# An adaLN layer with gated linear attention and eight experts on one core: expert rows scattered home, tiles in pairs, packed projections

## The chip, the cores and the metric

One of the eight cores of a Trainium2 chip runs the whole program. The metric is the time of one execution in microseconds of the device (us), shorter being better. Engines are called as the profile calls them: PE (matrix products), PEld (its weight loads), DVE, ACT and POOL (elementwise work), SP (issues transfers). All data are 32-bit floats, and each matrix product appears as two records in the trace.

## The reference

Input `x` is (2, 1024, 256). With a modulation `mod` of a small vector `c`:

```python
mod = (_silu(L0_c) @ L0_wmod).reshape(L0_c.shape[0], 6, 1, -1)
ga = (2 * (ga >= 0) - 1) * jnp.maximum(jnp.abs(ga), 0.25)   # gb likewise
x = x + ga * attn(_layernorm(x) * (1 + ca) + sa)
x = x + gb * ffn(_layernorm(x) * (1 + cb) + sb)
```

`attn` is gated linear attention: 16 heads of 16, chunks of 64 tokens, projections q, k, v, an output gate, and decay gates `log_sigmoid(x @ Wg1 @ Wg2 + bg2) / 16` of low rank 16. `ffn` routes each token to the best two of 8 experts (width 176, `silu(h1) * h2` between `up` and `proj`), weighs their results by softmax probabilities, and adds a shared expert of width 704 times a sigmoid gate.

## The kernel before, in words

Tokens stand in 16 tiles of 128, four tiles to a block of 512. The text calls the pass `s` of the main loop a slot. Five stages follow each other.

1. **Attention (slots 0 to 4).** Slot `s` projects block `s` (G the output gate, V, K, Q) and makes block `s-1`'s scores, masks, outputs and output projection (WO), block `s-2`'s layer norm, transposes (HT) and router. Near its end a slot transposes the next block, makes its low-rank product (LR, lines 1222 and 1352) and its gate logits (Z, line 1357), then the key-value sums (KV, line 1395). The products of a slot go through two PSUM banks, `work0` and `work1`, in turn: `unit_order` lists the units, and `begin` makes PE wait until the unit two before has been read. Scores go to four banks `at_ps`, outputs to `o_even` and `o_odd`. DVE masks the scores (line 978) and ACT evacuates and makes the exponentials.
2. **Shared expert.** For a block the parts are six "up" parts (line 1192: units SA and SB, two products of 512 columns each; the sixth has only 64 hidden features) and two "down" parts (line 1202). `FILL_PLACES` puts the parts of blocks 0 to 2 into gaps of slot 4 and of the routing.
3. **Routing and scatter.** DVE computes for each token and choice a row in a table sorted by expert (`pos_u`, line 822), each expert's rows filled up to whole tiles of 128. POOL writes `h2tok` rows to those places in DRAM with 32 indirect transfers (line 523). Meanwhile PE works off the remaining shared parts (the place "scatter").
4. **Experts.** 40 tiles of 128 sorted rows are loaded back in pairs (SP, line 400). For each tile PE transposes the rows (line 1494), makes both up products with the weights of the tile's expert, which it reads by a register (line 1510, 352 columns), transposes the hidden values (line 1518, two halves of 88) and multiplies down (line 1525, 256 columns, 88 rows of the array). DVE copies the result (line 1121) and SP stores it, still sorted, to `ys_sorted` (line 406).
5. **Tail.** POOL gathers two rows for each token (line 532, 32 indirect transfers), DVE weighs and adds them (lines 1159 to 1168), and SP stores the tile (line 421). PE makes block 3's whole shared part beside it.

```python
            pe.wait_ge(y_out, ETILES)
            for f in range(FTS):
                shared_up(pe, t_, begin, NBLK - 1, f)
```

At the start POOL clears `vpad` and `atm` (lines 437 and 438), then makes the masks, and signals `const_pool` behind the last (line 471). PE waits for it ahead of its first transposes (line 1346).

## Time and profile before

| | |
|---|---|
| median of three runs | 502.7 us (502.02 to 503.12) |
| the profiled execution's own time | 501.09 us |
| its span, first to last instruction | 499.1 us |
| PE busy | 433.5 us, 87% of the span |
| DVE, ACT, POOL busy | 238.8, 137.4, 110.1 us |
| mean granted clock of PE | 0.921 of full |

The engines run side by side and wait for each other by semaphores, so a busy share does not tell what ends last. A stage is read by its windows, its waits and the chain of waits that ended last. The span is 2.0 us shorter than the execution's time, for what lies around it.

### The profile page before, as it was taken

The page shows a single profiled execution, that of the slowest core. Times are in us where ns is not written, and L with a number is a line of the kernel's source. Part 1 is how long each engine was busy: PE and PEld are TensorE (multiplying, and loading weights), DVE is VectorE, ACT ScalarE, POOL GpSimd, SP SyncE. Part 2 cuts the span into 40 slices and gives each one's busy share as a digit, 9 for nine tenths or more (in the row PEclk, how much of TensorE's full clock was granted, in tenths as well). Part 3 has the DMA queues.
Part 4 walks back from the last instruction along what each step waited for, and adds up shares of the span by engine and source line. Part 5 has one row for each costly group of instructions (what it writes and reads, how often), then busy time and mean ns, then how long its engine had stood idle before and what let it go on. Part 6 is the DMA issues. An engine that isn't in the chain of part 4 may idle for free.

```text
span 499.1 us, 9641 instructions
## 1 busy us (share of the span) xinstructions
PE 433.5 (87%) x3860; PEld 269.4 (54%) x3861; DVE 238.8 (48%) x573; ACT 137.4 (28%) x277; POOL 110.1 (22%) x134
## 2 busy tenths in 40 slices
PE   2798799999999998997999896758999999997466
PEld 2344465558456666634645642525777777752134
DVE  4054395487749569112543621021444444437467
ACT  2285413643743521161113110002222222210000
POOL 9203000510321051010000177700000000027742
PEclk9989878979988998799999999956999999998869
DMA  8990000000000000092000022330242434225533
GB/s 281 319 385 11 3 3 3 0 3 4 3 1 4 3 1 3 3 255 94 0 0 1 11 95 105 106 105 0 87 125 89 123 90 120 75 73 147 148 95 95
DMA packets 31248, 38.29 MB, mean 77 GB/s; under 512 B 3481, under 2 KB 28394, under 8 KB 31210
## 3 DMA queue, kind: packets, MB, share of 16 engines
q1 hardware_dynamic: 28138, 29.35, 18.7%
q0 software_dynamic: 3072, 8.39, 5.4%
q8 instruction: 29, 0.48, 0.4%
q14 instruction: 9, 0.07, 0.1%
HBM read 20.95 MB, written 16.78 MB: 76 GB/s over the span
## 4 chain that ended last, share of the span: by engine, by line
PE 68%; DVE 11%; issue 6%; ACT 5%; POOL 5%; another core or an unknown queue 3%; DMA 1%; DVEq 0%; POOLq 0%
PE work L1192 11%; PE at_ps L1510 10%; PE work L1222 8%; PE work L1525 7%; PE work L1202 7%; PE at_ps L1255 4%; PE work L1380 3%; PE work L1337 3%; PE at_ps L1494 2%; PE at_ps L1243 2%; PE work L1357 2%; PE o_even L1305 1%; PE work L1328 1%; PE work L1395 1%
## 5 line engine op out<-in xcount | busy, mean ns | idle before, releaser
L1202 PE MATMUL work<-sdn_sb,hs 128*128 128x256 f32 x192 | 52.8, 420 | 12.5 <-issue 6.7
L1510 PE MATMUL at_ps<-arena 128*128 x160 | 56.8, 478 | 1.3 <-ACT arena L748 1.1
L1202 PEld LDWEIGHTS work<-sdn_sb,hs 128*128 128x128 f32 x192 | 36.2, 202 | 30.2 <-issue 16.9
L523 POOL DMA_INDIRECT xs_sorted<-h2tok,pos_u x32 | 31.3, 979 | 73.5 <-DVE pos_u L822 64.1
L900 DVE TENSOR_TENSOR hs<-work,hs 128x512 f32<-128x512 f32 (+1 forms) x24 | 16.5, 689 | 64.0 <-PE work L1192 39.8
L1192 PE MATMUL work<-h2T,sup_sb 128*128 128x512 f32 (+1 forms) x96 | 45.1, 619 | 0.6 <-DVE hs L900 0.3
L532 POOL DMA_INDIRECT er_neg<-ys_sorted,pos_u x16 | 15.5, 969 | 128.5 <-DMA ys_sorted<-er_pos 119.7
L1525 PE MATMUL work<-arena 88*128 x160 | 41.1, 380 | 0.0
L545 ACT ACTIVATE hs<-work 128x512 f32<-128x512 f32 (+1 forms) x24 | 14.3, 596 | 90.4 <-PE work L1192 61.3
L1510 PEld LDWEIGHTS at_ps<-arena 128*128 128x128 f32 x160 | 31.1, 196 | 13.6 <-issue 3.5
L1192 PE MATMUL work<-hT,sup_sb 128*128 128x512 f32 (+1 forms) x48 | 25.5, 680 | 14.3 <-DVE hs L900 11.8
L752 ACT ACTIVATE arena<-at_ps 128x176 f32<-128x176 f32 x40 | 12.7, 318 | 77.2 <-PE at_ps L1510 77.2
L486 POOL TENSOR_TENSOR sq<-sq,sg 128x512 f32<-128x512 f32 x8 | 10.0, 1274 | 101.2 <-issue 101.2
L1192 PEld LDWEIGHTS work<-h2T,sup_sb 128*128 128x128 f32 (+1 forms) x96 | 17.2, 187 | 24.8 <-issue 22.4
L1525 PEld LDWEIGHTS work<-arena 88*128 88x128 f32 x160 | 27.2, 190 | 2.4 <-issue 0.2
L1192 PEld LDWEIGHTS work<-hT,sup_sb 128*128 128x128 f32 (+1 forms) x48 | 9.1, 201 | 29.4 <-issue 15.0
L1255 PE MATMUL at_ps<-arena 32*64 32x128 f32 x512 | 22.1, 349 | 2.8 <-issue 1.6
L748 ACT ACTIVATE arena<-at_ps 128x256 f32<-128x256 f32 x40 | 15.4, 384 | 30.3 <-PE at_ps L1494 30.1
L1192 PE MATMUL work<-za,sup_sb 128*128 128x512 f32 (+1 forms) x48 | 21.0, 596 | 1.3 <-DVE tmp L908 1.3
L908 DVE SCALAR_TENSOR_TENSOR tmp<-work,sgate,rows 128x256 f32<-128x256 f32 x16 | 7.0, 479 | 31.1 <-remote 19.8
L1121 DVE COPY er_pos<-work 128x256 f32<-128x256 f32 x40 | 17.0, 425 | 9.4 <-PE work L1525 9.4
L1222 PE MATMUL work<-hT,wgate_sb 128*128 128x512 f32 x32 | 20.8, 808 | 0.7 <-ACT za L622 0.7
(196 smaller groups left out, 730.8 us busy)
## 6 DMA issues: line engine op xcount, KB each, us to landing
xs_sorted<-arena SPq DMA_DIRECT2D x10, 512.0 KB, 7.8
h2tok<-xs_sorted SPq DMA_DIRECT2D x20, 256.0 KB, 2.8
ys_sorted<-er_pos SPq DMA_DIRECT2D x20, 256.0 KB, 2.2
arena<-in_e_up SPq DMA_DIRECT2D x8, 352.0 KB
x_sb<-in_x SPq DMA_DIRECT2D x4, 512.0 KB, 8.5
out_rows<-xn SPq DMA_DIRECT2D x16, 128.0 KB
sup_sb<-in_s_up SPq DMA_DIRECT2D x1, 1408.0 KB, 6.4
arena<-in_e_down SPq DMA_DIRECT2D x8, 176.0 KB
```

What stands on the lines that cost most here:

```text
L523: g.indirect_dma_start(out=xs_dram, out_offset=bass.IndirectOffsetOnAxis(ap=pos_u[:, k, t:t + 1], axis=0), in_=h2tok[:, t, :], in_offset=N ...
L532: g.indirect_dma_start(out=gath_sb[k][:, t % 4, :], out_offset=None, in_=ys_dram, in_offset=bass.IndirectOffsetOnAxis(ap=pos_u[:, k, t:t + ...
L748: a.activation(xT[:, u % 2, :], at_ps[u % 2][:, 0:KC * P], ACT.Copy).then_inc(xT_ready, 1)
L900: v.tensor_tensor(hs[0:m, f, :], bank(("SB", blk, f))[0:m, :], hs[0:m, f, :], ALU.mult).then_inc(hs_ready, 1)
L1121: v.tensor_copy(yout[:, (u // 2) % 2, u % 2, :], work[u % 2][:, 0:HID]).then_inc(y_out, 1)
L1192: ins = t_.matmul(o[0:m, :], sup_sb[:, k, w, f0:f0 + m], h2T_of[blk][:, k, :], start=(k == 0), stop=(k == KC - 1))
L1202: ins = t_.matmul(o[:, t * HID:(t + 1) * HID], hs[0:m, f, tk], sdn_sb[0:m, f, :], start=(f == 0), stop=(f == FTS - 1))
L1222: ins = t_.matmul(o[0:rows_, :], w[:, k, gr * P:gr * P + rows_], rhs[:, k, :], start=(k == 0), stop=(k == KC - 1))
L1255: ins = t_.matmul(at_ps[j][CHUNK * e:CHUNK * (e + 1), q * P:(q + 1) * P], kh[r, gr, c * CHUNK:(c + 1) * CHUNK], qeo[r, gr, c, :, :].rearra ...
L1337: ins = t_.matmul(o[:, t * HID:(t + 1) * HID], hT[:, k, tk], wv_sb[:, k, :], start=(k == 0), stop=(k == KC - 1))
L1510: ins = t_.matmul(at_ps[2 + u % 2][:, 0:2 * FE], xT[:, u % 2, k * P:(k + 1) * P], eup[:, bass.ds(e, 1), k, :].rearrange("p a n -> p (a n)" ...
L1525: ins = t_.matmul(work[u % 2][:, 0:HID], hTe[0:FEH, u % 2, k * P:(k + 1) * P], edn[0:FEH, bass.ds(e, 1), k, :].rearrange("p a n -> p (a n) ...
```

## The change

It has nine parts. Line numbers of code after it are those of the changed file.

1. **Start.** POOL makes the identity first and signals it by itself (`ident_ready`). PE's first transposes wait for that alone. `vpad` and `atm` are cleared behind `const_pool`. SP issues more small loads (four copies of `wg2`, two of `bg2`) and the shared up weights in four transfers.
2. **Packed LR and Z.** LR is four products of 32 weight columns, each in its own quarter of the output rows. Z is two products of 64 array rows each, one per half of the array. Z goes to `at_ps[2]` and `at_ps[3]` and is no longer a unit of `work`.
3. **Block order.** Half of G now stands ahead of the first scores, and V ahead of HT. The modulation rows of batch 0 are finished in slot 0 and those of batch 1 in slot 2.
4. **Packed sixth up part.** SA and SB of the last 64 features are one product of 128 columns.
5. **Four early up parts.** Four of block 3's six up parts move from the tail to the place "scatter".
6. **Wider rows.** A sorted row has 263 numbers in place of 256. Among the seven more are its token, its weights and its batch. The probabilities are made ahead of the positions.
7. **Pairs of expert tiles, 39 of 40.** Hidden transposes of two tiles fill one bank and are copied at once. The down product is split into 128 and 48 rows of the array in place of twice 88. For the second tile of a pair the 48 rows stand at 64 to 111, with weights that ACT copies there.
8. **Scatter home.** POOL computes each sorted row's place from its extra columns (five small operations per pair), DVE multiplies the expert's result by the token's weight and the `gb` row while it copies it out of PSUM, and POOL writes it to its token's row with one indirect transfer per tile.
9. **Tail.** SP loads both tables of rows back, eight transfers of 512 KB. DVE adds two times per pair of token tiles and SP stores.

```diff
-    both("Z", 0)
@@ main loop, PE
             for s in range(NBLK + 1):
+                if s < NBLK:
+                    project(("G", s, 0), wgate_sb, 0, hT)
                 if b >= 0:
                     scores_first(b)
                 if s < NBLK:
-                    for gr in range(KC):
-                        project(("G", s, gr), wgate_sb, gr, hT)
+                    project(("G", s, 1), wgate_sb, 1, hT)
@@ low_rank, gate_logits
-                project(("LR", s, 0), wg1_sb, 0, hT, LOWR)
+                for gr in range(KC):
+                    for k in range(KC):
+                        r = slice(32 * (2 * gr + k), 32 * (2 * gr + k) + 32)
+                        ins = t_.matmul(o[r, :], wg1_sb[:, k, :], hT[:, k, :], start=True, stop=True)
-                    o = begin(("Z", s, gr))
-                    t_.matmul(o[:, :], wg2_sb[:, gr * P:(gr + 1) * P], tT[:, :], start=True, stop=True).then_inc(unit_full, 1)
+                    r = slice(64 * gr, 64 * gr + 64)
+                    t_.matmul(at_ps[2 + gr][:, :], wg2_sb[r, gr * P:(gr + 1) * P], tT[r, :], start=True, stop=True
+                              ).then_inc(z_full, 1)
@@ shared_up
+            if f == FTS - 1:
+                o = begin(("SA", blk, f))
+                for k in range(KC):
+                    ins = t_.matmul(o[:, :], sup_tail[:, k, :], h2T_of[blk][:, k, :],
+                                    start=(k == 0), stop=(k == KC - 1))
+                return
@@ fill and tail
+EARLY_UP = 4
+SHARED_PARTS += [("U", NBLK - 1, f) for f in range(EARLY_UP)]
-            for f in range(FTS):
+            for f in range(EARLY_UP, FTS):
                 shared_up(pe, t_, begin, NBLK - 1, f)
@@ experts, PE
+            def down(i, q, w, e, tiles=2):
+                pe.wait_ge(hTe_ready, q + 1)
+                at_least(pe, y_out, i, 0)
+                for t in range(tiles):
+                    t_.matmul(work[t][:, 0:HID], hTe[:, w % 2, t * P:(t + 1) * P],
+                              edn[:, 0, bass.ds(e[t], 1), :].rearrange("p a n -> p (a n)"), start=True, stop=False)
+                ins = t_.matmul(work[0][:, 0:HID], hTe[0:FE1, w % 2, 2 * P:3 * P],
+                                edn[0:FE1, 1, bass.ds(e[0], 1), :].rearrange("p a n -> p (a n)"), start=False, stop=True)
+                if tiles == 2:
+                    pe.wait_ge(odd_ready, q + 1)
+                    r = slice(CHUNK, CHUNK + FE1)
+                    ins = t_.matmul(work[1][:, 0:HID], hTe[r, w % 2, 3 * P:4 * P], edn_odd[r, w % 2, :],
+                                    start=False, stop=True)
@@ experts, POOL
+            def put_rows(q):
+                for u in range(min(2, ETILES - 2 * q)):
+                    i = 2 * q + u
+                    pool.wait_ge(y_out, i + 1)
+                    g.indirect_dma_start(out=ys_dram, out_offset=bass.IndirectOffsetOnAxis(ap=goal_u[:, i:i + 1], axis=0),
+                                         in_=yout[:, q % 2, u, :], in_offset=None, bounds_check=TOPK * TOK - 1,
+                                         oob_is_err=False).then_inc(ys_stored[i % 4], 16)
+            for q in range(EPAIRS):
+                if q + 2 < EPAIRS:
+                    goals(q + 2)
+                put_rows(q)
@@ experts, DVE
+            def row_gains(i, u):
+                    v.scalar_tensor_tensor(out=row_gain[:, t, :], in0=row_step, scalar=goal[:, (u // 2) % XPAIRS, t, 2:3],
+                                           in1=rows[:, 0, GB, :], op0=ALU.mult, op1=ALU.add).then_inc(gain_ready, 1)
+            def evac_y(i0, q0, u):
+                dve.wait_ge(down_full, q0 + u // 2 + 1)
+                dve.wait_ge(gain_ready, i0 + u + 2 - u % 2)
+                v.scalar_tensor_tensor(out=yout[:, (u // 2) % 2, u % 2, :], in0=work[u % 2][:, 0:HID],
+                                       scalar=goal[:, (u // 2) % XPAIRS, u % 2, 1:2], in1=row_gain[:, u % 2, :],
+                                       op0=ALU.mult, op1=ALU.mult).then_inc(y_out, 1)
@@ tail, SP and DVE
+            for q in range(NBLK):
+                for k in range(TOPK):
+                    r0 = k * TOK + q * BLK
+                    sp.dma_start(yin[:, q, k, :, :], ys_dram[r0:r0 + BLK, :].rearrange("(t p) c -> p t c", p=P)
+                                 ).then_inc(ld_y[q], 16)
+            def combine(n):
+                t = 2 * n
+                steps.did(v.tensor_tensor(y0, y0, y1, ALU.add))
+                xv = x_sb[:, t:t + 2, :]
+                v.tensor_tensor(xv, y0, xv, ALU.add).then_inc(comb_done, 2)
```

**Where a slot turns over, PE.** Before, from LR's neighbour to the outputs from the state (`hT,wg_sb` is LR, `tT,wg_sb` is Z, `arena,xn` is KV, `at_ps<-arena` the scores, `wgate_sb` G):

```order
L1222 MATMUL work<-hT,wg_sb 16x512 x2
L1380 MATMUL work<-wo_sb,yT 128x256 x4
L1357 MATMUL work<-tT,wg_sb 128x512 x2
L1395 MATMUL work<-arena,xn 32x32 x64
L1255 MATMUL at_ps<-arena 64x128 x32
L1222 MATMUL work<-hT,wgate_sb 128x512 x4
```

After:

```order
L1463 MATMUL work<-hT,wg_sb 32x512 x4
L1499 MATMUL work<-wo_sb,yT 128x256 x4
L1475 MATMUL at_ps<-tT,wg_sb 128x512 x2
L1514 MATMUL work<-arena,xn 32x32 x64
L1325 MATMUL work<-hT,wgate_sb 128x512 x2
L1360 MATMUL at_ps<-arena 64x128 x32
L1325 MATMUL work<-hT,wgate_sb 128x512 x2
```

LR has four products in place of two, Z leaves `work`, and half of G has come between KV and the scores.

**One expert tile, PE, before** (`ISA` reads a register; `arena` holds weights and hidden values):

```order
L1510 ISA
L1510 MATMUL at_ps<-arena 128x352
L1510 ISA
L1510 MATMUL at_ps<-arena 128x352
L1494 MATMUL at_ps<-ident,h2tok 128x128 x2
L1518 MATMUL o_even<-ident,arena 88x128 x2
L1525 ISA
L1525 MATMUL work<-arena 128x256
L1525 ISA
L1525 MATMUL work<-arena 128x256
```

After, half of a pair's turn (up of the second tile, its successor's transposes, the down products of the pair in front):

```order
L1630 MATMUL at_ps<-arena 128x352
L1630 ISA
L1630 MATMUL at_ps<-arena 128x352
L1614 MATMUL at_ps<-ident,h2tok 128x128 x2
L1648 REGISTER_ALU
L1651 ISA
L1651 MATMUL work<-arena 128x256
L1651 ISA
L1651 MATMUL work<-arena 128x256
L1653 ISA
L1653 MATMUL work<-arena 128x256
L1658 MATMUL work<-xn,arena 128x256
```

Four down products serve two tiles as before, but the last two stand on different halves of the array. The hidden transposes of both tiles (lines 1640 and 1643) stand once per pair, ahead of this piece.

**The same stage, POOL, after** (before, POOL has nothing there); one pair's goals, then two scatters of the pair two before:

```order
L565 TENSOR_SCALAR second<-h2tok,texp 128x1 [waits ld_xt3]
L565 TENSOR_SCALAR second<-h2tok,texp 128x1
L568 TENSOR_TENSOR turned<-h2tok,second 128x6 [waits pool_step]
L571 TENSOR_TENSOR goal<-turned,h2tok 128x6 [waits pool_step]
L574 TENSOR_SCALAR goal_u<-goal 128x2 [waits goal_ready]
L582 DMA ys_tokens<-er_pos,goal_u 4096x256 [waits y_out,pool_step]
L582 DMA ys_tokens<-er_pos,goal_u 4096x256 [waits y_out]
```

Five small operations and two indirect transfers per pair have moved into a stage in which POOL was idle.

**The tail, DVE.** Before, one token tile behind one of block 3's up parts:

```order
L900 TENSOR_TENSOR hs<-work,hs 128x512 [waits unit_full,silu_done]
L1159 TENSOR_SCALAR er_neg<-er_neg,pw 128x256 [waits out_stored0,gath0]
L1161 SCALAR_TENSOR_TENSOR er_neg<-gk,pw,er_neg 128x256 [waits dve_step]
L1163 TENSOR_TENSOR er_neg<-er_neg,rows 128x256 [waits dve_step]
L1168 TENSOR_TENSOR xn<-er_neg,x_sb 128x256 [waits dve_step]
```

After, the last two up parts and the first four token tiles:

```order
L984 TENSOR_TENSOR hs<-work,hs 128x512 [waits unit_full,silu_done]
L984 TENSOR_TENSOR hs<-work,hs 64x512 [waits silu_done]
L1263 TENSOR_TENSOR arena<-arena 128x512 [waits ld_y0]
L1269 TENSOR_TENSOR x_sb<-arena,x_sb 128x512 [waits dve_step]
L1263 TENSOR_TENSOR arena<-arena 128x512
L1269 TENSOR_TENSOR x_sb<-arena,x_sb 128x512 [waits dve_step]
```

Four operations per token tile have become two per pair of tiles, and they wait for loads instead of gathers.

## Rows read from the trace of the kernel before

**Rows 1.** The page: the span, and GB/s moved in its 40 equal slices.

```profile
span 499.1 us, 9641 instructions
...
GB/s 281 319 385 11 3 3 3 0 3 4 3 1 4 3 1 3 3 255 94 0 0 1 11 95 105 106 105 0 87 125 89 123 90 120 75 73 147 148 95 95
```

**Rows 2.** Windows of six stages: length, then busy us (instructions) of PE, PEld, DVE, ACT, POOL, clock, DMA.

```profile
0.00:61.40 61.40, 43.84 (x305) 23.19 (x306) 21.38 (x47) 28.84 (x46) 18.37 (x38) 0.95 0.61 203
61.40:107.30 45.90, 42.76 (x717) 26.82 (x709) 31.35 (x60) 18.19 (x34) 8.54 (x10) 0.83 0.01 2
...
211.60:284.80 73.20, 67.98 (x224) 37.47 (x224) 28.59 (x89) 19.90 (x31) 2.49 (x2) 1.00 0.21 60
284.80:336.40 51.60, 37.93 (x97) 19.30 (x97) 10.36 (x18) 3.58 (x6) 31.33 (x32) 0.85 0.30 102
336.40:442.30 105.90, 104.16 (x480) 77.57 (x480) 43.72 (x120) 24.39 (x80) 0.00 (x0) 0.96 0.29 87
442.30:499.10 56.80, 37.48 (x96) 17.52 (x96) 33.57 (x76) 3.58 (x6) 31.23 (x32) 0.88 0.40 116
```

**Rows 3.** Waits of PE over the span: waiter <- releaser: total us, times, longest.

```profile
PE work L1346 <- POOL qsel L471: 5.3, 1, 5.3
...
PE work L1395 <- ACT za L622: 2.2, 3, 0.7
PE work L1395 <- issue: 2.0, 1, 2.0
...
PE at_ps L1255 <- DVE arena L978: 1.1, 1, 1.1
```

**Rows 4.** Timeline of PE in slots 2 and 3: start, us, engine, line, x records.

```profile
99.66 1.98 PE L1357 MATMUL work<-tT,wg_sb 33*128 33x512 f32 x4
...
107.27 4.84 PE L1222 MATMUL work<-hT,wgate_sb 128*128 128x512 f32 x8
...
113.95 2.59 PE L1255 MATMUL at_ps<-arena 32*64 32x128 f32 x64
...
140.35 1.89 PE L1222 MATMUL work<-hT,wg_sb 128*16 128x512 f32 x4
```

**Rows 5.** Timeline of PE, shared parts of 64 and of 128 weight columns.

```profile
224.72 3.17 PE L1192 MATMUL work<-h2T,sup_sb 128*64 128x512 f32 x7
...
247.08 8.85 PE L1192 MATMUL work<-h2T,sup_sb 128*128 128x512 f32 x20
```

**Rows 6.** Timeline of the fill stage: POOL's first and last scatter, SP's loads, PE.

```profile
284.85 1.21 POOL L523 DMA_INDIRECT xs_sorted<-h2tok,pos_u  x1 [64.09 <-DVE pos_u L822]
...
324.66 0.96 POOL L523 DMA_INDIRECT xs_sorted<-h2tok,pos_u  x1 [0.30 <-issue]
...
327.09 1.91 SPq L400 DMA_DIRECT2D h2tok<-xs_sorted  x4
...
328.93 0.58 PE L1202 MATMUL work<-sdn_sb,hs 128*128 128x256 f32 x1 [0.82 <-issue]
...
330.33 4.08 PE L1202 MATMUL work<-sdn_sb,hs 128*128 128x256 f32 x8 [0.82 <-issue]
```

**Rows 7.** Chain that ended last, in order of time, one expert tile.

```profile
436.48 0.86 PE work L1525 x4
437.35 1.19 PE at_ps L1510 x4
```

**Rows 8.** Lines with their shapes, 347.8 to 437.3 us: 36 tiles.

```profile
L1121 DVE COPY er_pos<-work 128x256 f32<-128x256 f32 x36 | 15.3, 425 | 7.9 <-PE work L1525 7.9
```

**Rows 9.** Lines of POOL over the span: a small operation.

```profile
L495 POOL TENSOR_TENSOR f_all<-f_base,f_last 128x16 f32<-128x16 f32 x4 | 0.9, 220 | 0.0
```

**Rows 10.** Timeline of the tail: DVE behind its longest wait, POOL beside DVE, DVE's last.

```profile
477.16 0.69 DVE L900 TENSOR_TENSOR hs<-work,hs 128x512 f32<-128x512 f32 x1 [8.20 <-remote]
...
486.45 1.15 POOL L532 DMA_INDIRECT gk<-ys_sorted,pos_u  x1 [0.30 <-issue]
```

**Rows 11.** Timeline of DVE: the last instruction before the last store.

```profile
495.69 0.69 DVE L921 TENSOR_TENSOR xn<-x_sb,tmp 128x512 f32<-128x512 f32 x1
```

More of the change, by code:

```diff
@@ L387, in _ @@
             sp.wait_ge(zero_ready, 5)
-            for i in range(ETILES // 4):
+            for i in range(ESLOTS // 4):
                 sp.dma_start(xs_dram[i * BLK:(i + 1) * BLK, :].rearrange("(t p) c -> p t c", p=P),
@@ L461, in _ @@
                                           base=0, pattern=[[0, 2 * NPAIR], [1, CHUNK]], channel_multiplier=-1))
+            for j in range(0, NPAIR, 2):
+                steps.sync()
+                steps.did(g.affine_select(out=lr_bias[:, :], in_=lr_bias[:, :], compare_op=ALU.not_equal, fill=1.0,
+                                          base=-(32 * j + LOWR), pattern=[[0, 1]], channel_multiplier=1))
             steps.sync()
@@ new lines, in _ @@
+            dve.wait_ge(y_ready, 2 * NBLK)
+            steps.did(v.tensor_tensor(row_step, rows[:, 1, GB, :], rows[:, 0, GB, :], ALU.subtract))
+            steps.sync()
+            group(0, 0, first=True)
+            with dve.Fori(1, ESLOTS // EGRP - 1) as grp:
+                group(grp * EGRP, grp * XPAIRS)
+            group(ESLOTS - EGRP, ESLOTS // 2 - XPAIRS, tiles=ETILES - ESLOTS + EGRP)
+            evac_hT(EPAIRS - 1, XPAIRS - 1)
+            row_gains(ETILES - 1, EGRP - 2)
+            y_slot_free(ESLOTS - EGRP, EGRP - 2)
```

489 lines of the change are left out of this document (273 added, 216 removed).

## Prediction

> **What bounds the kernel now.** I read the page for the span, then the windows by stage, then in each stage the waits, the timeline and the chain. The span is 499.1 us [rows 1]. The windows say where it goes [rows 2]: slots 0 and 1 (61.4 and 45.9 us), the routing after slot 4 (73.2), the fill (51.6), the experts (105.9) and the tail (56.8). PE is busy 104.16 of 105.9 us in the experts, 67.98 of 73.2 in the routing and 42.76 of 45.9 in slot 1, so there PE's own work sets the time. It is busy only 37.93 of 51.6 in the fill and 37.48 of 56.8 in the tail, at clocks of 0.85 and 0.88: these two stages wait. In the fill POOL issues scatters from 284.85 to 325.6 and SP loads the sorted rows from 327.09 [rows 6]. But PE is late too: at 328.93 it still makes the last down part, with 0.58 us per product record and idle time put down to "issue". In the tail POOL is busy 31.23 of 56.8 us with gathers, and DVE once waits 8.20 us for something that the profile cannot name [rows 10]. So four stages are to be judged by themselves, and the gains of stages in series add up.
>
> **The attention slots.** Part 1 takes away PE's wait for POOL's masks, 5.3 us [rows 3]. Nothing is queued there that could take its place: the small loads that SP now issues ahead are needed only after the first transposes. Bound from 3 to 5.3, I take 5.3.
>
> Part 2: LR and Z are four records each, 1.89 and 1.98 us [rows 4], though LR has 16 weight columns and Z 33 array rows, so narrowness alone saves nothing. Packed, LR is eight records in four quarters and Z four in two halves; side by side each lasts as long as two records, 0.95 us. Are they side by side? The scores say so: 64 records of 128 columns in 2.59 us are 0.040 us each [rows 4], while four records of 352 columns take 1.19 us [rows 7], which for 128 columns is 0.108 us each. That is 2.7 at a time. So I take 0.95 us off each of the eight (four blocks, two each), 7.6 in all. The bounds are 0 and 7.6.
>
> The Trainium skill, TensorEngine Tiling, section Key Properties, says the opposite can happen: changing the tiling mode drains TensorE. By that rule, with one drain per change, the packing could give back what it wins, and this is a rival below; the trace, with its dense scores, speaks for the gain.
>
> Part 3: KV no longer follows Z in the same banks, so its waits go: 2.2 us for ACT and 2.0 put down to issue [rows 3]. The modulation rows leave slot 1, where scores waited 1.1 us for DVE [rows 3]. Against this, half of G (four records, the eight of rows 4 took 4.84 us at a falling clock) now stands ahead of the scores, and DVE's masks start later by that. DVE is busy 31.35 of 45.9 us there [rows 2], much of it behind the scores. I give back 1 us in each of three slots. Sum: 5.3 + 7.6 + 2.2 + 2.0 + 1.1 - 3 = 15.2 us. The bounds are 6 (no packing gain, more given back) and 20.
>
> **Routing.** Part 4 drops four records for each block. Seven records of 64 weight columns take 3.17 us, 0.45 each, and twenty of 128 columns 8.85, 0.44 each [rows 5]; so width is free and 1.8 us goes per block. Blocks 0 and 1 stand ahead of the positions: 3.6 us. The probabilities now come ahead of the positions, but DVE waits there for PE's counts, so I cost them at nothing; uncovered, six operations of about 0.2 us are 1.2. The first scatter then starts at 284.85 - 15.2 - 3.6 = 266.0.
>
> **The fill.** Two floors. The scatters: 42.2 us from the first to the loads [rows 6], plus 1 MB of loads at 281 GB/s [rows 1], 3.7; together 46. A row of 1,052 bytes in place of 1,024 changes nothing here, since DMA engines are busy 0.30 of the stage [rows 2] and POOL's issue, 0.96 us and 0.30 before it, sets the pace. PE: an up part is eight records of 0.44, 3.5 us; a down part is 24, at 4.08/8 us each for half clock [rows 6], so 0.25 at full, 6.0. The place held three down and six up parts, 39 us, of which the first down part, 6.0, is done when the scatter starts; now it holds three down and 9.5 up, 51.3. Before, 51.6 us passed over 33 us of work: 19 us were lost, 2 of them the turn to the experts. With none lost the stage lasts 51.3 - 6.0 = 45, with all of it 64. Part of the loss was at the end, while the scatters and the loads ran, and would now lie elsewhere in PE's work. I take the middle, 55: the experts start at 321. The early parts are thus nearly free here, and what they cost if the scatters were no cover is 4 x 3.5 = 14 us, which the tail gives back.
>
> **The experts.** 36 tiles take 347.8 to 437.3 us [rows 8], 2.49 each, 4.97 a pair. Of it down is 0.86 per tile [rows 7]. The pair's two 48-row products stand on different halves and banks: four records in the time of two, 0.43 less, 4.54. The first two stay full. The transposes and ACT's copy of the odd weights change nothing: the copy's target is read a pair later. Nineteen pairs and one tile: 88.8. The stage before had 105.9 - 99.6 = 6.3 us for a cold start and its end; PE now comes to it warm, so 3.5. Stage 92.3, ending at 413.3.
>
> Whether others keep up: DVE has per pair two copies of 0.43 [rows 8] in their new form, two row gains alike, one copy of 512 columns (0.69 by [rows 11]) and two products of at most 0.43, 3.3 us of 4.54. POOL has two transfers of 1.26 and five operations of 0.22 [rows 9], 3.6 us with no gaps, 5.1 with 0.3 before each. It is the nearest to the bound. Who waits: DVE's copy for the slot that POOL empties, PE's next down product for that copy. Beside a busy DVE a transfer took 1.15 us in place of 0.96 [rows 10, 6]: 0.4 more for a pair, 4.0, still under 4.54.
>
> The Trainium skill, DMA: Bandwidth & Descriptors, section SWDGE vs HWDGE vs iDMA, has DVE lock GpSimd out of the memory that holds the descriptor rings during two-port operations. That is in line with the 1.15, and by it POOL's part would grow further than by the row.
>
> **The tail.** After the last copy: one scatter 0.96 and its landing 1.5 (325.62 to 327.09) [rows 6], 2.5; issue and first landing, 2 as an estimate from the same landing; 4.2 MB of loads, with 1.6 MB of stores among them, at 350 GB/s (between the 281 and 385 of [rows 1]) 16.6; the last block's two pairs of DVE operations, 4 x 0.69 [rows 11], 2.8; two last additions of the shared part, 2 x (0.43 + 0.43 + 0.69), 3.1; the last store, 499.1 less 496.4 [rows 1, 11], 2.7. Sum 29.8 in place of 56.8. PE's own work beside it, 1.5 up parts and two down parts, is 17 us and hidden. Bounds: 26 (loads at 385, stores free) and 36 (all at 250).
>
> **Sum.** 413.3 + 29.8 = 443.1 for the span. The profiled execution took 2.0 us more than its span, and the median of the runs stands 1.6 us above it (502.7 against 501.1). Forecast 447 us.
>
> **Rivals.** (A) Packing does not overlap, since each change between whole and divided array empties PE. Then eight times 0.95 and twenty times 0.43 are not saved, 16 us: 463. The scores speak against it; that they hardly ever leave the divided form speaks for it. Chance 0.12. (B) PE's losses in the fill vanish, since the rest of its work lies behind the last scatter. The experts then start at 312 to 314: 439. For it: the slow records stand at the end of the scatters. Chance 0.20. (C) POOL paces the experts at 5.1 to 5.9 us per pair, 12 to 27 us more: about 466. For it, the rows just named; against, small operations at 0.22 with nothing before them [rows 9]. Chance 0.10. (D) Slower than before: the landing of the scatters holds the two result slots. A slot is free when copy 0.9, two issues 2.5 and the landing L are over, and that has two pairs' time, 9.1 us; so it is hidden up to L = 5.7, and each microsecond more costs 0.5 per pair, 10 in all. With 55 us to lose it decides from L = 11. The landing seen is 1.5 [rows 6]. Price at L = 12: 510. Chance 0.04. (E) The new block order costs DVE's chain some 5 us in each slot: 462. Chance 0.04. Mine has 0.50, and 436 to 458 as its own range.
>
> **How the numbers follow.** Two runs of this kernel differ by some 0.2%, about 1 us, and I call that "same". All cases but (D) end far below 502.7. The range from 431 to 470 takes in A, B, C and E; it leaves out D and the far ends. Faster 0.94, same 0.01, slower 0.05.
>
> **What would show it.** Right: first transposes 5 us earlier; LR and Z of 1 us; first scatter near 266; experts from about 321 with 4.5 us per pair and no idle PE; last up part to last store 30 us. Wrong: a pair of 4.97 (A); DVE's copies released by POOL or by transfers (C, D); PE waiting for DVE's masks (E); or loads of 512 KB landing one after the other far below 300 GB/s in the tail.

## The result, and the profile after

Beside each other the changed kernel took 457.0 us (median of 6 runs, 452.9 to 459.1) and the kernel before 502.9 (501.5 to 508.6). The ratio is 0.907, with an interval of 0.901 to 0.913: 46 us less, where the forecast had 447 us and 56 less. Ratios, here and below, leave out a few executions with a lower granted clock that are over 1.5% longer than the fastest of their kernel, so they need not be the quotient of the medians. The profiled execution took 459.1 us over a span of 457.3; the forecast's span was 443.1. So 14.2 us are to be explained on the span, and, as the experiments show, some of it depends on the chip that the program runs on.

The page of the changed kernel, to be read against [rows 1]:

```profile
span 457.3 us, 9813 instructions
...
GB/s 262 296 309 240 3 5 1 3 3 4 0 3 4 1 1 4 2 268 114 0 0 0 2 47 106 107 106 106 0 83 105 89 122 97 84 92 47 32 313 238
```

The last two slices of GB/s are the loads and stores of the tail. Its windows, columns as in [rows 2], cut at the same points of the program as the later ones of [rows 2]: the fill in three pieces, and the tail.

```profile
266.00:286.00 20.00, 19.43 (x46) 8.27 (x45) 6.69 (x12) 2.98 (x5) 14.59 (x15) 1.00 0.25 88
286.00:313.00 27.00, 12.76 (x49) 8.61 (x48) 0.98 (x2) 0.59 (x1) 17.25 (x19) 0.80 0.35 117
313.00:331.00 18.00, 17.16 (x36) 7.56 (x36) 5.45 (x10) 2.69 (x6) 4.18 (x15) 0.83 0.08 27
...
430.00:457.30 27.30, 19.55 (x62) 11.28 (x61) 15.63 (x25) 1.19 (x2) 1.94 (x2) 0.91 0.72 234
```

The second piece of the fill is the one to look at: PE is busy 12.76 of 27 us, DVE 0.98, ACT 0.59, while POOL and the transfers go on as before. The timeline of that stretch, against [rows 6] (the stop of DVE first, then PE's slow records, then the loads; in brackets the idle time ahead and what ended it, "remote" being what the profile can't name):

```profile
286.84 0.69 DVE L984 TENSOR_TENSOR hs<-work,hs 64x512 f32<-64x512 f32 x1 [1.57 <-issue]
...
287.59 11.15 PE L1305 MATMUL work<-sdn_sb,hs 128*128 128x256 f32 x45 [1.41 <-DVE hs L984]
...
304.25 0.58 PE L1305 MATMUL work<-sdn_sb,hs 64*128 64x256 f32 x1 [2.32 <-issue]
...
309.83 21.57 SPq L421 DMA_DIRECT2D h2tok<-xs_sorted  x5
312.71 0.88 DVE L992 SCALAR_TENSOR_TENSOR tmp<-work,sgate,rows 128x256 f32<-128x256 f32 x2 [25.18 <-remote]
...
313.64 16.73 PE L1295 MATMUL work<-hT,sup_sb 128*128 128x512 f32 x32 [8.81 <-DVE tmp L992]
...
331.23 1.15 PE L1630 MATMUL at_ps<-arena 128*128 x3 [0.43 <-ACT arena L802]
```

PE has the first down part's 24 records done by 293.6, so DVE could copy then. It does so at 312.71, 2.9 us after SP's first load of sorted rows is issued. PE's last three records of the second part end 0.8 to 2.9 us apart in place of 0.25 (each lasts 0.4 to 0.6, the rest is idle time ahead of it), and then its next bank waits for DVE. All 32 records of the early up parts stand behind that, 313.64 to 330.2. The experts start at 330.2, not at 321.

What did DVE wait for in those 19 us? The chain of waits over the same stretch (start, us, what) says that it was a signal, and when the signal came:

```profile
286.88 25.81 another core or an unknown queue
312.69 0.03 issue
312.71 0.89 DVE tmp L992 x2
```

The signal at 312.69 is an update of the semaphore `unit_full`, by which PE reports a finished unit. The trace holds the time of each such update: in all 14 traces DVE's copy of block 2's first down part starts 0.02 to 0.03 us behind one. In c1 below, where nothing stands still, it comes at 291.60, with the end of PE's 24th record. Here it comes 19.1 us after that record, and the one for the second down part, whose last record ended at 304.83, follows at 312.91. So DVE was ready, and PE's signal came late by these records.

PE in one pair of expert tiles, against [rows 7]:

```profile
345.86 1.35 PE L1630 MATMUL at_ps<-arena 128*128 x4
...
347.26 1.03 PE L1651 MATMUL work<-arena 128*128 x4
348.22 0.48 PE L1653 MATMUL work<-arena 48*128 x1
348.23 0.48 PE L1658 MATMUL work<-xn,arena 48*128 48x256 f32 x1
348.54 0.38 PE L1653 MATMUL work<-arena 48*128 x1
348.55 0.38 PE L1658 MATMUL work<-xn,arena 48*128 48x256 f32 x1
348.85 1.45 PE L1630 MATMUL at_ps<-arena 128*128 x4
...
350.80 1.35 PE L1630 MATMUL at_ps<-arena 128*128 x4
```

From one L1630 at 345.86 to the same point a pair later at 350.80 it is 4.94 us; 4.54 was forecast and 4.97 was the figure of before. The packed records L1653 and L1658 do start together, 10 ns apart. There is no idle time between records.

The chain of waits at the end, in order of time (start, us, engine, what), against [rows 10, 11]:

```profile
431.80 2.09 DMA ys_tokens<-er_pos,goal_u
...
439.49 8.87 DMA arena<-ys_tokens
```

### The profile page after: what moved, and what is told of

The parts are those of the page before. It is cut to its first block, busy times and chain, and to the rows that moved or that the text cites. A ratio compares the mean times of both kernels' runs of the same rounds, so it can differ in the third digit from the quotient of the medians.

```text
span 457.3 us, 9813 instructions
## 1 busy us (share of the span) xinstructions
PE 401.1 (88%) x3848; PEld 245.4 (54%) x3849; DVE 238.7 (52%) x559; ACT 146.0 (32%) x295; POOL 147.7 (32%) x249
## 4 chain that ended last, share of the span: by engine, by line
PE 70%; DVE 8%; ACT 6%; another core or an unknown queue 6%; issue 4%; DMA 4%; SPq 1%; DVEq 0%; POOLq 0%; ACTq 0%
PE work L1295 13%; PE at_ps L1630 11%; PE work L1325 7%; PE work L1305 4%; PE work L1651 4%; PE work L1499 4%; PE at_ps L1360 3%; PE work L1653 3%; PE work L1445 3%; DMA arena<-ys_tokens 2%; PE at_ps L1348 2%; PE at_ps L1614 2%; PE work L1436 2%; PE o_even L1413 2%
## 5 line engine op out<-in xcount | busy, mean ns | idle before, releaser
L582 POOL DMA_INDIRECT ys_tokens<-er_pos,goal_u x39 | 43.8, 1123 | 44.3 <-DVE er_pos L1218 38.5
L1630 PE MATMUL at_ps<-arena 128*128 x156 | 54.5, 472 | 0.4 <-ACT arena L802 0.4
L984 DVE TENSOR_TENSOR hs<-work,hs 128x512 f32<-128x512 f32 (+1 forms) x24 | 16.6, 692 | 63.8 <-PE work L1295 50.4
L1295 PE MATMUL work<-h2T,sup_sb 128*128 128x512 f32 x80 | 37.9, 623 | 0.6 <-DVE hs L984 0.3
L1630 PEld LDWEIGHTS at_ps<-arena 128*128 128x128 f32 x156 | 26.5, 190 | 14.9 <-issue 6.6
L1295 PE MATMUL work<-hT,sup_sb 128*128 128x512 f32 x40 | 22.1, 719 | 9.4 <-DVE tmp L992 8.8
L1218 DVE SCALAR_TENSOR_TENSOR er_pos<-work,goal,sq 128x256 f32<-128x256 f32 x39 | 17.1, 480 | 21.3 <-PE work L1658 20.6
L1295 PEld LDWEIGHTS work<-h2T,sup_sb 128*128 128x128 f32 x80 | 15.2, 197 | 19.7 <-issue 17.4
L992 DVE SCALAR_TENSOR_TENSOR tmp<-work,sgate,rows 128x256 f32<-128x256 f32 x16 | 7.0, 479 | 34.0 <-remote 25.2
L1062 DVE COPY_PREDICATED arena<-causal,at_ps 128x512 f32<-128x512 uint32 x32 | 20.5, 714 | 5.4 <-PE at_ps L1360 5.4
L1197 DVE TENSOR_TENSOR arena<-at_ps,arena 128x176 f32<-128x176 f32 x39 | 13.3, 342 | 19.0 <-ACT arena L806 18.0
L1651 PE MATMUL work<-arena 128*128 x78 | 20.3, 382 | 2.4 <-DVE arena L1203 2.4
L1295 PEld LDWEIGHTS work<-hT,sup_sb 128*128 128x128 f32 x40 | 9.1, 232 | 22.9 <-issue 11.4
L1499 PE MATMUL work<-wo_sb,yT 128*128 128x256 f32 x64 | 17.0, 418 | 3.2 <-DVE yT L1079 2.9
L1325 PE MATMUL work<-hT,wgate_sb 128*128 128x512 f32 x32 | 16.6, 648 | 3.4 <-DVE kv_in L1102 3.4
L1445 PE MATMUL work<-wv_sb,hT 128*128 128x256 f32 x64 | 15.9, 391 | 3.1 <-ACT sg L735 1.7
```

What stands on the lines that cost most here:

```text
L582: g.indirect_dma_start(out=ys_dram, out_offset=bass.IndirectOffsetOnAxis(ap=goal_u[:, i:i + 1], axis=0), in_=yout[:, q % 2, u, :], in_offs ...
L984: v.tensor_tensor(hs[0:m, f, :], linear, hs[0:m, f, :], ALU.mult).then_inc(hs_ready, 1)
L1062: v.copy_predicated(atm[:, n % 2, j, :], causal[:, :, :].bitcast(U32).rearrange("p r l -> p (r l)"), at_ps[j][:, :]).then_inc(atm_ready, 1)
L1218: v.scalar_tensor_tensor(out=yout[:, (u // 2) % 2, u % 2, :], in0=work[u % 2][:, 0:HID], scalar=goal[:, (u // 2) % XPAIRS, u % 2, 1:2], in ...
L1295: ins = t_.matmul(o[0:m, :], sup_sb[:, k, w, f0:f0 + m], h2T_of[blk][:, k, :], start=(k == 0), stop=(k == KC - 1))
L1325: ins = t_.matmul(o[:, :], w[:, k, gr * P:(gr + 1) * P], rhs[:, k, :], start=(k == 0), stop=(k == KC - 1))
```

## Experiments

Twelve kernels ran, in three groups, each on one chip: I call them chip A (the runs a1 to a4), chip B (b1 to b4) and chip C (c1 to c4). The kernel before ran on each beside them: 501.2, 490.6 and 491.2 us.

**a1: no early up parts.**

```
-EARLY_UP = 4
+EARLY_UP = 0
```

> The four early up parts go back behind the experts. In the changed kernel DVE stood still from 293.5 (first down part of block 2 ended on PE) to 312.71 us, and PE ran the early parts only after that, 313.64 to 330.20, 16.6 us. Theory 1 (the early parts are paid in full, since the stop of DVE ends only with the scatters and loads): the experts start 14 to 16 us earlier, near 316, and the tail grows by only what its own cover of 17 us of PE work leaves open: PE's 31 us against 27 us now, 4 to 8 us more; the whole is 7 to 11 us faster, near 448. Theory 2 (the forecast's: the fill is a cover and early parts use it): the experts start at most 5 us earlier, and the tail gives back as much or more; the whole is the same or slower.

Measured: 460.8 us (459.1 to 464.4), ratio to before 0.924 (0.915 to 0.932). DVE's copy stood 25.21 us again, to 313.42. PE's first expert rows, and PE behind the last expert tile:

```profile
317.07 1.08 PE L1614 MATMUL at_ps<-ident,h2tok 128*128 128x128 f32 x4 [12.91 <-issue]
```

```profile
420.55 17.43 PE L1295 MATMUL work<-hT,sup_sb 128*128 128x512 f32 x40 [0.63 <-DVE er_pos L1218]
```

The start of the experts fits Theory 1 (317.07, 13 us earlier), the total does not: up parts after the experts begin at 420.55 in place of 431.08 and hold five of 3.4 us in place of one, so nearly all that came in front is given back behind. From the first scatter to the end it is 190.5 us here and 190.2 in the changed kernel. With the stop present, doing the four parts early wins nothing that I could measure.

**a2: the 48-row products one after the other.**

```
-                    m = CHUNK * t + FE1
+                    m = FE1
...
-                    ins = t_.matmul(work[1][:, 0:HID], hTe[r, w % 2, 3 * P:4 * P], edn_odd[r, w % 2, :],
+                    ins = t_.matmul(work[1][:, 0:HID], hTe[0:FE1, w % 2, 3 * P:4 * P],
+                                    edn[0:FE1, 1, bass.ds(e[1], 1), :].rearrange("p a n -> p (a n)"),
```

> The 48-row product of the second tile of each pair stands on rows 0 to 47 again, as that of the first; nothing runs side by side, no quarter or half of the array is named in the experts' loop. Theory 1 (packing wins 0.43 us per pair and something else in the new loop loses as much): a pair takes 5.35 us in place of 4.94, and the kernel is 8 us slower. Theory 2 (the two products do overlap, 0.21 us each, but each change to and from the halved array costs about 0.1 us, three records of 0.96, 0.63 and 1.29 in place of 0.87, 0.43 and 1.19): a pair takes 4.97 to 5.0, and the kernel is slower by 0.5 to 1 us at most, hardly to be measured.

Measured: 466.9 us (462.5 to 469.9), ratio 0.931 (0.923 to 0.940), 6 us above a4 (460.5, below), which is the changed kernel but for 64 small writes; their ranges overlap, and 8 were expected. One pair on PE:

```profile
350.03 1.03 PE L1651 MATMUL work<-arena 128*128 x4
350.99 0.70 PE L1653 MATMUL work<-arena 48*128 x2
351.53 0.59 PE L1657 MATMUL work<-arena 48*128 x2
352.05 1.45 PE L1630 MATMUL at_ps<-arena 128*128 x4
...
355.40 1.03 PE L1651 MATMUL work<-arena 128*128 x4
```

A pair takes 355.40 - 350.03 = 5.37 us, at the upper of the two clock levels as in the changed kernel's trace: Theory 1. Packing wins the 0.43 that I gave it (5.37 to 4.94); what I had missed is that the other cut of the 176 rows, 128 and 48 in place of 88 and 88, costs 0.40 by itself. Where it lies shows when the same stretch is asked for record by record:

```profile
350.68 0.38 PE L1651 MATMUL work<-arena 128*128 x1
350.99 0.48 PE L1653 MATMUL work<-arena 48*128 x1
351.31 0.38 PE L1653 MATMUL work<-arena 48*128 x1
352.45 0.46 PE L1630 MATMUL at_ps<-arena 128*128 x1
```

Inside a form the records start 0.22 us apart, whether they have 48 rows (351.31 to 351.53), 128 rows (the first four) or, in the kernel before, 88. Into the 48-row form the two steps are 0.31 and 0.32, and out of it 0.31 (from 351.74 to 352.05) and 0.40, where L1630 otherwise has 0.30. So it is not the number of rows that costs: each change of form costs 0.20, in two steps of 0.10, and a pair has two changes, 0.40. The rule of the Trainium skill (TensorEngine Tiling, Key Properties), that a change of the tiling mode drains TensorE, agrees with this, and 0.20 us is its price here. Packing saves two steps inside the form, 0.43, and leaves both changes in place.

The kernel before pays the same price in its down parts of the shared expert, where 24 records take 6.0 us in place of 24 times 0.22: these too go from 128 to 64 rows and back. The price could have been read there before the change.

**a3: half of the scatters.** It leaves out the scatters of the second choices, as its expectation says.

```
-            for k in range(TOPK):
+            for k in range(1):
```

> Leaves out the 16 scatters of the second choices (half of the rows of the sorted table stay zero, and the sum at the end reads the first choices twice). Read only up to the first expert. Theory S (DVE and PE need new program code in this stretch, and its delivery is held up as long as scatters are in flight, wherever in the scatters the place falls): the stop of DVE disappears, for the scatters end near 286 before the place is reached; PE then works through, down parts 287 to 300, early parts to 314, experts from 315. Theory T (a backlog that builds up after some 17 scatters): the same, so this run alone does not tell S from T. Theory N (nothing to do with the scatters, a fixed wait at this place of the program): DVE still stands until about 312.

Measured, in the fill alone (DVE's copy, then PE):

```profile
295.81 0.88 DVE L992 SCALAR_TENSOR_TENSOR tmp<-work,sgate,rows 128x256 f32<-128x256 f32 x2 [6.13 <-PE work L1305]
```

```profile
289.74 12.00 PE L1305 MATMUL work<-sdn_sb,hs 128*128 128x256 f32 x48 [1.41 <-DVE hs L984]
...
315.50 0.60 PE L1614 MATMUL at_ps<-ident,h2tok 128*128 128x128 f32 x4
```

On the same chip A there is no stop and no slow record when the last scatter is issued at 289.1: Theory N falls. The stop of the changed kernel is bound to the scatters or to what follows them: here POOL has the first loaded rows at 295.10 already, ahead of PE's signal at 295.78. It is one execution.

**a4: DVE's program shifted by 64 instructions.**

```
             steps = Steps(dve, dve_step)
+            for i in range(64):
+                v.memset(shift_pad[:, i:i + 1], 0.0)
```

> 64 writes of one column each stand at the head of DVE's program, in its idle time before the first input, some 4 us there; every later instruction of DVE thus stands 64 further on in its program. Theory S (the stop is where DVE's program code runs out and the delivery of more waits for the scatters): DVE's stop at 293 to 312 moves or goes away, and the down parts' copies follow PE within 1 us; if PE's own slow records (298.7 to 304.8) stay, the experts start 5 to 8 us earlier, near 324. Theory T (a backlog of the scatters reaches DVE's signals after some 17 scatters): the stop stays where it is, experts at 330 to 331, time within 1 us of the changed kernel.

Measured: 460.5 us (457.8 to 464.2). The stop is 25.16 us long and ahead of the same copy:

```profile
318.17 0.88 DVE L995 SCALAR_TENSOR_TENSOR tmp<-work,sgate,rows 128x256 f32<-128x256 f32 x2 [25.16 <-remote]
```

So Theory S, in the form in which the place is fixed by a count of instructions, falls. The changed kernel's trace speaks against late program code altogether: between 292 and 339 us it has no packet on a queue of instructions (one of 16 KB starts at 290.3), so none arrives when DVE goes on. The Trainium skill (Runtime: NRT & Kernel Launch, Instruction fetch mechanics) calls the crossing of a 16 KiB block of program mostly hidden; no run here shows a stop at a place that such a count would fix.

**b1: small writes ahead of the copy that stood still.**

```
+                if (blk, jj) == (NBLK - 2, 0):
+                    for i in range(48):
+                        v.memset(probe[:, i:i + 1], 0.0)
                 wait_unit(dve, ("SD", blk, jj))
```

> 48 writes of one column each, which wait for nothing, stand on DVE behind the last product of block 2's up parts and ahead of the copy that stood still for 25.2 us. Theory R (DVE's instructions arrive late while scatters are in flight): the small writes are themselves held up, either at once at 287 or part of the way through, at a point that tells how many DVE had in hand. Theory G (the instructions are there, and the signal of PE that the copy waits for arrives late): all 48 run by 291 and DVE is silent from there to 312. The total is within 1 us of the changed kernel either way, so this run is also the changed kernel's time beside the next three.

Measured: 440.3 us (437.7 to 441.8), with 490.6 for the kernel before on this chip, ratio 0.906 (0.890 to 0.922). The stop was gone: all 48 small writes ran within 0.75 us from 287.09, and the copy followed at 293.27 behind PE. So this run puts neither theory to the test. The late signal in the traces that have the stop speaks for Theory G.

**b2 and b3: scatters held back.** In b2 with four semaphores in turn (c3 is the same kernel on chip C); in b3 by a pause in the middle.

```
+                    n = k * NTILE + t
+                    if n >= 4:
+                        pool.wait_ge(xs_landed[n % 4], 16 * (n // 4))
```

```
+                if k:
+                    pool.wait_ge(shev_done, 2 * (NBLK - 1))
                 for t in range(NTILE):
```

> Scatter n of the sorted rows waits until scatter n-4 has landed. Theory T (a backlog of rows on their way builds up after some 17 scatters and holds PE and DVE): the interval of 1.27 us between scatters stretches from about the 17th on, the stop of DVE disappears, and the experts start at 315 to 320 in place of 331. Theory U (no backlog: each scatter lands 1.5 us after its issue; what holds DVE and PE is the mere presence of scatters): interval 1.27 throughout, stop of 25 us as before, experts at 331, total unchanged within 1 us.

> POOL stops between the scatters of the first and of the second choices until DVE has the copies of block 2's second down part. The run with half of the scatters showed no stop. Theory 1 (the stop needs scatters in flight at the time of the event): DVE's copies follow PE at 293.6 and 299.6, POOL goes on at 300.5 and ends at 321, loads at 322.5 to 325.5, and the experts start at 326 to 328, 3 to 5 us earlier than in the changed kernel, unless a new stop comes in the second half, while the early up parts run. Theory 2 (the stop is tied to the number of scatters, some 17 to 25, wherever they stand): PE or DVE stops in the second half instead, until 325, and the experts start at 331 or later.

Measured: b2 444.5 us (439.9 to 445.8), the first scatter at 268.99 and the last at 309.27, 1.3 us apart as ever: no backlog of four. Without a stop on this chip the run says nothing on whether one would have been cured. b3 457.8 us (450.6 to 460.7; its profiled execution is the one of 450.6, against 441.8 for b1's): the pause of 12.8 us is paid, since PE then waits 12 us for the sorted rows. Neither of its two theories was put to the test.

**b4: LR and Z not packed.**

```
-                for gr in range(KC):
-                    for k in range(KC):
-                        r = slice(32 * (2 * gr + k), 32 * (2 * gr + k) + 32)
-                        ins = t_.matmul(o[r, :], wg1_sb[:, k, :], hT[:, k, :], start=True, stop=True)
+                for k in range(KC):
+                    ins = t_.matmul(o[0:32, :], wg1_sb[:, k, :], hT[:, k, :], start=(k == 0), stop=(k == KC - 1))
...
-                    r = slice(64 * gr, 64 * gr + 64)
+                    r = slice(0, 32)
```

> Low rank and gate logits without packing: two accumulating products on 32 columns of the array for LR, and both halves of Z on the same 32 rows, one after the other. If the packing is worth what the records say (LR 1.89 against 1.00, Z 1.98 against 1.06 to 1.11, four blocks, all on the critical path): 0.89 + 0.9 = 1.8 us per block, 7.2 in all, first scatter 7 us later than in the changed kernel, and the kernel 7 us slower. If the switches of the array between its whole and its divided form cost as much in the records around them, or the slots wait for something else: 0 to 2 us.

Measured: 445.9 us (444.4 to 447.7), 5.6 above b1 and 1.4 above b2 on the same chip, so by the totals the packing is worth some 1 to 6 us. Locally it is plain. The changed kernel's second slot, and the same place in b4:

```profile
82.24 1.06 PE L1463 MATMUL work<-hT,wg_sb 128*32 128x512 f32 x8
...
85.16 1.13 PE L1475 MATMUL at_ps<-tT,wg_sb 64*128 64x512 f32 x4
86.22 1.31 PE L1514 MATMUL work<-arena,xn 64*32 64x32 f32 x128
88.92 0.70 PE L1325 MATMUL work<-hT,wgate_sb 128*128 128x512 f32 x1 [1.39 <-DVE kv_in L1102]
```

```profile
82.61 1.90 PE L1461 MATMUL work<-hT,wg_sb 128*32 128x512 f32 x4
...
86.37 1.98 PE L1473 MATMUL at_ps<-tT,wg_sb 32*128 32x512 f32 x4
88.28 1.32 PE L1512 MATMUL work<-arena,xn 64*32 64x32 f32 x128
90.36 0.90 PE L1325 MATMUL work<-hT,wgate_sb 128*128 128x512 f32 x1 [0.76 <-DVE kv_in L1102]
```

From LR's start to KV's it is 3.98 us packed and 5.67 not, 1.69 less. Behind KV a wait for DVE's copy grows from 0.76 to 1.39 us, and 0.6 of the 1.7 goes back: 1.1 us net in this slot. Over the four blocks it is best read at a like granted clock: with a mean of 0.97 up to there, the first up part of the routing stretch starts at 168.91 (c3), 169.63 (b3) and 169.96 (a1) with the packing, and at 173.50 here. So packing is worth 3.5 to 4.6 us, against 7.2 by the records.

**c1 to c4: the changed kernel as it is, without early parts, with four in flight, and the kernel before.** c1 and c4 have no edit; c2 has those of a1 and b1, c3 that of b2.

> The changed kernel as it is, for a trace beside the next three on one chip. On the chip of a1 to a4, and on that of the first result, DVE stood 25.2 us in the fill; on the chip of b1 to b4 it did not, though b4 had that stretch unchanged. Theory C (the stop belongs to the chip on which the program runs, not to the kernel): either the stop of 25.2 us with experts at 330 to 332, or none with experts at 313 to 317, and all four kernels of this call show the same of the two. Theory K (the small edits of b1 to b4 removed it): the stop is there in this kernel and gone in c2 and c3.

> No early up parts, and the 48 small writes of b1. With the stop present, a1 showed that the early parts win nothing: experts 14 us earlier, tail 14 us longer. Without the stop: PE ends the down parts at 301, but the sorted rows land only at 312, so the experts start at 313 to 315 with or without early parts, and the tail is 14 us longer: the kernel 12 to 14 us slower than c1. If the stop is present, the small writes tell whether DVE lacks instructions (they are held up) or the signal (all run at 287 to 291).

> At most four scatters in flight, as b2. With the stop present in c1: Theory T (a backlog holds PE and DVE) has it gone or much shorter here, experts at 315 to 320, 10 us faster than c1; Theory U (the mere presence of scatters) has it unchanged. Without the stop in c1: same time as c1 within 3 us, scatter interval 1.27 us as in b2.

> The kernel before, for its trace on this chip. With the stop: PE's slow records and the copy that stood 19.8 us, experts at 336 to 338. Without: PE works through the fill, nine parts from the first scatter, the sorted rows land at 42.2 + 3.7 us after it, so the experts start 46 to 47 us after the first scatter, near 332, only 5 us earlier. So the whole change is worth more where there is no stop.

Measured: c1 441.3 us (440.1 to 445.3), ratio to before 0.900 (0.895 to 0.906); c2 456.5 (454.2 to 459.4), ratio 0.928; c3 439.9 (436.2 to 441.7), ratio 0.897; c4 489.9, one run, its experts 45.1 us behind the first scatter (46 to 47 expected). PE in the fill of c1, unmodified:

```profile
285.55 12.00 PE L1305 MATMUL work<-sdn_sb,hs 128*128 128x256 f32 x48 [1.41 <-DVE hs L984]
297.47 14.00 PE L1295 MATMUL work<-hT,sup_sb 128*128 128x512 f32 x32
311.31 0.60 PE L1614 MATMUL at_ps<-ident,h2tok 128*128 128x128 f32 x4
```

and of c4, the kernel before:

```profile
306.88 12.00 PE L1202 MATMUL work<-sdn_sb,hs 128*128 128x256 f32 x48 [0.84 <-DVE hs L900]
329.28 0.69 PE L1494 MATMUL at_ps<-ident,h2tok 128*128 128x128 f32 x2 [10.40 <-DMA h2tok<-xs_sorted]
```

The same program has the stop on one chip and not on another: Theory C, as far as four groups can tell, since each group also had its own time and its own program load. The traces differ in one more thing. Of the 512 landing signals of the scatters, those of the first result and of chip A hold 145 to 151, in the kernel before as in the changed one (a3, with 256 to hold, has 104 and no stop); those of chips B and C hold 508 to 512. So where the stop is, the trace itself is short of records. Each execution has a span and a granted clock on record, so none ran without being recorded, and whether the recording itself holds PE's signals back is not tested.

In the kernel before the stop had shown as well. These are its waits for something that the profile can't name, five in all, in the trace that the prediction was made from; the trace of c4 has none of them, and that of c1 none either:

```profile
DVE tmp L908 <- remote: 19.8, 1, 19.8
...
ACT hs L545 <- remote: 18.4, 2, 12.1
...
DVE hs L900 <- remote: 14.3, 2, 8.2
```

And c2 shows what the early parts are worth where PE isn't stopped. Its first expert rows wait for their loads:

```profile
314.23 1.11 PE L1618 MATMUL at_ps<-ident,h2tok 128*128 128x128 f32 x4 [13.36 <-DMA h2tok<-xs_sorted]
```

The sorted rows land 45.8 us after the first scatter (268.41) whether PE is busy or not, so without early parts PE idles 13.4 us, and the kernel is 15 us slower. Of the 17.1 us between the two profiled spans 3.3 stand ahead of the first scatter, where the kernels are alike, so the early parts are worth some 14.

c4 also puts the losses of [rows 6] right. Without a stop the kernel before still takes 45.1 us from its first scatter to the experts, as PE waits 10.40 us for the sorted rows; with it, 51.5. The stop cost that kernel 6.5 us in the fill, and the rest of what PE idled there was the wait for rows.

## Why the prediction was right, and where it was off

The median of 457.0 lies in the range (431 to 470) and at the upper edge of my own case (436 to 458). The span, term by term, is 443.1 + 1.1 (first scatter) + 8.1 (fill) + 8.5 (experts) - 3.5 (tail) = 457.3.

**Slots: right in sum, in part by luck.** The first 128-column up part of the routing stretch stands at 171.95, at 186.62 before: 14.7 us earlier, 15.2 forecast. Of the terms, the start gave 4.3 of 5.3 (the first transposes stand at 11.4 us, 15.8 before), and the packing 3.5 to 4.6 of 7.6 (b4): 1.7 us per block in its own records, less what went to a longer wait for DVE's copy. That is some 8 us. Most of the rest is a term that the forecast doesn't have, the granted clock. Up to this point it was 0.92 in the kernel before and 0.96 after, which is 30 and 14 us at the lower level. What such time costs can be estimated from a2 and c3, which have the same code up to the first scatter: it stands at 269.06 with a mean of 0.94 and at 261.10 with 0.97, 8 us for some 16 at the lower level. So about 8 of the 14.7 us came with the clock, and part 3, with 2.3 forecast, cost 1 or 2. The changed kernel had 0.93 to 0.97 up to the first scatter, the kernel before 0.93 in both of its traces; how much of this gain the change brings and how much the execution is open.

**Routing: a little less.** POOL's first scatter is at 267.14 against 284.85, 17.7 earlier in place of 18.8. A packed sixth part lasts 1.88 us, which is what I took. The 266.0 of the forecast was met within 1.1 us, while the same code has its first scatter anywhere from 261.1 to 269.3.

**The fill: the step that failed.** "I take the middle, 55": it lasted 267.14 to 330.20, 63.1, so nearly all of the 19 us of losses stayed (64 was the bound "with all of it"), and on chips B and C none did: 265.10 to 311.31 in c1, 46.2, as my floors had it: PE's own work ended then (45 forecast), 0.4 us behind the landing of the rows (46). I had taken the losses of [rows 6] for something spread over PE's work that later work could dodge. The 19 were also the wrong size: I compared the stage with PE's work alone, though my other floor was 46. Beside c4, which has no stop, the kernel before had lost 6.5 us. The loss is one event: PE's signals come late and PE's records slow down while scatters are in flight, there or not there by the chip. In the changed kernel the early parts stand behind it, so it costs 16.8 us against c1: 14.1 until the early parts begin, and 2.7 in them, since the granted clock is 0.51 in their first 5.7 us. A middle between the two was the value that neither chip shows. On B and C the number of my rival B came out, 440.3 and 441.3 us against its 439, but not for its reason: there PE had no losses to move behind the last scatter.

**The experts: right mechanism, wrong base.** "Four records in the time of two, 0.43 less, 4.54. The first two stay full": packing did win 0.43, but against an unpacked pair of 5.37, not 4.97. The term that I set at nothing was the new cut of the rows, 0.40 per pair; over 19.5 pairs 7.8 of the 8.5 us. Rival A's 463 came nearer to the median of 457.0 than my 447 and had the cause only in part: the products overlap, and it is the two changes of form around them that cost, 0.20 each.

**POOL (rival C) and the landing (rival D)** didn't matter: POOL's 39 transfers took 1.12 us each and POOL waited 38.5 us for DVE's copies; DVE never waited for a landing. **Rival E** appears as 3.4 us of PE waiting for DVE's copy behind KV, three times, within the 14.7; b4, without the packing, has 2.2 us of it.

**The tail: each step seen.** From the last copy (431.02) to the first load 3.0 us (2.5 forecast), loads 434.03 to 448.39, 14.4 us, with a mean of 311 GB/s and 337 to 391 once they run (16.6 at 350 and 2 for the first landing forecast; 4.46 MB were moved in this time, hardly any of the 1.6 MB of stores that I had put among the loads), DVE 6.2 (5.9), the last store 2.7. 26.3 in place of 29.8. PE's own work there was 20.5 us, 431.08 to 451.6, not 17. It ended 3.2 us behind the loads, but DVE had its own additions to make until then and did not wait.

**The early parts.** "Nearly free here, and what they cost if the scatters were no cover is 14 us, which the tail gives back" holds in its first half only where there is no stop: on chip C the fill is 0.4 us longer with them (46.2 against 45.8), on chip A 13.8 (63.1 against 49.3). The tail gives back its part on both. So they are worth 14 to 15 us on chip C (c2), nothing measurable on chip A (a1).

What stays open: why PE's signals come late on some chips. Shown is that it needs the scatters or the loads behind them (a3), doesn't follow a count of DVE's instructions (a4), and was absent in all eight traces of chips B and C. Its end is tied to the scatters and loads and not to a place of the program: DVE goes on 45.6 to 45.7 us behind the first scatter in all five traces that have the stop, the kernel before among them, which is when the first sorted rows land (45.8 in c1). In the four of the changed kernel that is within 0.2 us of POOL's first operation on these rows. Whether four scatters in flight at most (b2) would cure it met no chip with the stop; c3 costs nothing (439.9 against 441.3), but that it helps is not shown. And no run tells the chip from the recording of the trace.

## What to carry to other kernels

When a trace has idle time that the profile can't name, take the same kernel's trace on a second chip before pricing a change against it: the stretch is then forecast with two values and a chance, never with their middle. When the cut of a contraction is changed so that parts of it can stand side by side, price the cut itself first, unpacked, since each change between the whole and the divided array cost 0.20 us here, however few rows the records had. Early work is worth the idle time that it fills, so ask what ends that idle time: here the landing of the rows on one chip, and a stop that the early work had to stand behind on another. And before a gain is put down to a change, compare the granted clock of both traces up to that point.

## What the runs showed of the hardware

- A stop of DVE of 25.2 us, four times within 0.1 us (25.18, 25.21, 25.26 and 25.16, the last of these with 64 more instructions ahead), of which 19 are beyond PE's work, while indirect scatters are in flight; PE's signal is recorded 19.1 us behind the end of its last record, and PE's next records end 0.8 to 2.9 us apart. It ends 45.6 to 45.7 us behind the first scatter. On two other chips, unmodified in c1, none of it is there.
- Matrix products of 256 columns start 0.22 us apart with 48, 88 or 128 rows. A change from 128 rows to 48 costs 0.20 us, and so does the change back. Two pairs of 48-row records, on different halves of the array, take 0.63 us side by side and 1.06 one after the other, both with the two changes; side by side they start 0.01 us apart.
- The same code reached its first scatter between 261.1 and 269.3 us, 8 us for some 16 more us at the lower clock level.
- The kernel before differs by 12 us between chips (502.7 and 501.2 against 490.6 and 491.2), and the changed kernel by 16; the ratios, 0.907 against 0.906 and 0.900, differ much less.
